# Building the per-batch matrix M four batches at a time, from stacked high and low weights, instead of in one fold per batch

## The chip, the core and the metric

The kernel runs on one core of one Trainium2 chip. The metric is the device time of one execution, in microseconds, as a median of several. Engines are called as the profile calls them: PE (TensorE) with PEld, its weight loads; DVE (VectorE); ACT (ScalarE); POOL (GpSimd); SP (SyncE), which issues every DMA here.

## What is computed

```python
ctx = x + _L0_xattn_ref(ctx_1024, _layernorm(x), fside, fside, ln1_w, ln1_b, ln2_w, ln2_b, Wq, Wkv, Wout)
#   q = ln2(layernorm(x)) @ Wq, scaled and shifted per head;  k, v = split(ln1(ctx_1024) @ Wkv)
#   out = softmax(q k^T / 8) v @ Wout,   16 heads of 64, 64 context rows per batch
y   = ctx + tanh(((_layernorm(ctx) @ W) @ A1) @ A2 + bias)
```

x is 16 batches x 1024 rows x 512, all float32. Each operand of a matmul is split in two float32r parts, high (`_hi`) and low (`_lo`), and a product is made of the passes high x high, high x low and low x high.

## The kernel before, in words

Once, in a setup, the weights are loaded and split, the three FFN matrices are multiplied into one (W3), and the keys and values of all 16 batches are computed and stored to DRAM (`kv_scratch`). For each batch b two matrices stand in SBUF: M = Wq K^T (512 x 1024, so that x M gives the scores of all heads at once) and N = V Wout (1024 x 512). Both are kept as high and low parts.

The work on x goes in slots. Slot t treats one tile of 128 rows, `m = t % 8` is its place in the batch, and there are T = 128 slots and three more to drain. In one slot PE does, in program order (`slot_pe`): the scores of tile t in two halves q = 0, 1, 12 matmuls of 128x512 each (`passes`, L153 and L158); the FFN of tile t-3, 12 matmuls (L153, L158, operands x2T and W3); and the product of the softmaxed scores of tile t-1 with N, two halves of 12 (L848, L855). That is 60 matmuls. Between the scores and their use lies a chain over all engines: DVE adds the bias (L923) and takes the maximum (L928), POOL subtracts it (L1021), ACT takes the exponential (L868), DVE sums (L934, L937), POOL normalises (L1028), SP stores the result to `p_scratch` (L782) and reads it back with rows and columns exchanged (`p_moved`, L791), DVE transposes 32x32 blocks (L949), ACT and DVE split into `pT_hi` (L873) and `pT_lo` (L954). The row tile after the attention goes a like way (`x2_scratch` L766, `x2_moved` L778, L961, L878, L970). Every queue runs its own program in order, and semaphores tie them together. SP is a queue like the others: a DMA that waits holds up all behind it.

Two slots of a batch do more. In slot m = 0, PE makes N of this batch (`fold_n_pe`, 24 matmuls), from the block-diagonal values in `bdv`. In slot m = 7, M of the next batch is made (`fold_m_pe`), strewn between the other matmuls: 16 chunks c, each of two head pairs, each pair one matmul of 256 columns (L658, Wq_hi with the high and low keys side by side) and one of 128 (L659, Wq_lo with the high keys), into one of four PSUM banks c % 4. ACT takes the high part out (L671) and copies the cross term (L670), DVE makes the rest (L681) and for odd chunks the low part (L684), POOL the low part of even ones (L691). PE may use a bank again only when these have read it (`m_bank_read`). There is one M buffer, so that the old M must be done with first. The keys are laid block-diagonally into `bdk` at m = 4, the values into `bdv` at m = 6 (L609, L618, L600).

Slots 0 to 2 and the last 8 stand written out; the 15 x 8 between them are a hardware loop over batches (`run`, L1055), with DMA addresses and wait values from registers.

```python
            for t in range(3):
                slot(eng, t, t)
            with eng.Fori(0, B - 1) as b:
                for j in range(3, TPB + 3):
                    slot(eng, b * TPB + j, j % TPB)
            for t in range(T - 5, T + 3):
                slot(eng, t, t % TPB)
```

## Time and profile before

| | |
|---|---|
| median of 3 runs | 2175.47 us (2173.73 to 2175.64) |
| the profiled execution, its own time | 2175.19 us |
| its span | 2173.3 us |
| mean granted clock of PE | 0.989 |
| PE / PEld busy | 97% / 80% |
| DVE / ACT / POOL busy | 77% / 60% / 60% |
| DMA | 342.80 MB, mean 158 GB/s; share of the 16 engines 50.4% |

The span is what the profile covers; 1.9 us of the execution's own time lie outside of it. Two matmuls overlap in the records (each is shown with 0.39 us, though one starts every 0.227 us), so PE's pace is read from the starts, not from the durations.

### The profile page before, as it was taken

To read this page: it belongs to the slowest core of one execution; us is meant where nothing else is said; L and a number is where in the kernel's file an instruction comes from. 1 tells how busy PE (TensorE), PEld (TensorE's weight loads), DVE (VectorE), ACT (ScalarE), POOL (GpSimd) and SP (SyncE) were. 2 spreads that over 40 slices of the span, in tenths; PEclk is the share of its full clock that TensorE was granted. 3 is DMA by queue.
4 is the path that set the end of the run, shared out by engine and by line. 5 is a ranking of instruction groups with operands and counts; after the bars stand their busy time and mean duration, and the time that the engine had idled before them with its cause. 6 is when DMAs were issued, how large, how long until landed. Compare 5 with 4: busy or idle time off the path is not lost.

```text
span 2173.3 us, 35341 instructions
## 1 busy us (share of the span) xinstructions
PE 2104.7 (97%) x9632; PEld 1744.9 (80%) x9632; DVE 1678.3 (77%) x2778; ACT 1309.2 (60%) x3095; POOL 1306.3 (60%) x1460
## 2 busy tenths in 40 slices
PE   6977999999999999999999999999999999999997
PEld 5766888888888888888888888888888888888886
DVE  6746787878787787878878777878778787878875
ACT  3344666666666666666666666666666666665654
POOL 4433656656565666656565665756565666666564
PEclk8998999999999999999999999999999999999999
DMA  6422545555454544546464545546464555545453
GB/s 210 155 88 82 178 146 168 158 159 175 140 183 136 182 155 158 175 145 187 126 183 140 181 152 164 173 144 184 133 183 149 162 166 154 179 136 183 135 175 126
DMA packets 379887, 342.80 MB, mean 158 GB/s; under 512 B 72273, under 2 KB 269137, under 8 KB 379857
## 3 DMA queue, kind: packets, MB, share of 16 engines
q1 hardware_dynamic: 379856, 342.45, 50.4%
q8 instruction: 13, 0.21, 0.0%
q14 instruction: 18, 0.14, 0.0%
HBM read 199.62 MB, written 142.67 MB: 157 GB/s over the span
## 4 chain that ended last, share of the span: by engine, by line
PE 79%; issue 4%; ACT 4%; DVE 3%; POOL 2%; DMA 1%; SPq 0%; ACTq 0%; POOLq 0%; DVEq 0%
PE bank L153 31%; PE bank L848 19%; PE bank L158 15%; PE bank L855 10%; PE bank L658 3%; POOL area L1021 1%; ACT pT_hi L873 1%; PE bank L659 1%; DVE pT_lo L954 1%; ACT M_hi L671 1%; DVE row_max L928 1%; DVE turned L949 1%; ACT bank L718 1%; ACT area L670 0%; DMA p_moved<-p_scratch 0%
## 5 line engine op out<-in xcount | busy, mean ns | idle before, releaser
L1021 POOL TENSOR_TENSOR area<-area,row_max 128x256 f32<-128x256 f32 x512 | 360.2, 725 | 536.7 <-DVE row_max L928 536.7
L868 ACT ACTIVATE area<-area 128x512 f32<-128x512 f32 x256 | 162.0, 633 | 434.2 <-POOL area L1021 434.2
L1028 POOL TENSOR_TENSOR area<-area,row_inv 128x512 f32<-128x512 f32 x256 | 319.2, 1265 | 171.0 <-DVE row_inv L937 171.0
L848 PE MATMUL bank<-N_hi,pT_hi 128*128 128x512 f32 x1024 | 401.0, 392 | 4.1 <-ACT pT_hi L873 4.0
L153 PE MATMUL bank<-M_hi,xT_hi 128*128 128x512 f32 x1024 | 399.5, 390 | 0.0
L153 PE MATMUL bank<-M_lo,xT_hi 128*128 128x512 f32 x1024 | 399.2, 390 | 0.0
L848 PE MATMUL bank<-N_lo,pT_hi 128*128 128x512 f32 x1024 | 398.9, 390 | 0.0
L923 DVE SCALAR_TENSOR_TENSOR area<-bank,rs,area 128x512 f32<-128x512 f32 x256 | 192.0, 750 | 173.7 <-PE bank L158 170.5
L158 PE MATMUL bank<-M_hi,xT_lo 128*128 128x512 f32 x1024 | 274.8, 390 | 6.1 <-POOL xT_lo L745 5.9
L855 PE MATMUL bank<-N_hi,pT_lo 128*128 128x512 f32 x1024 | 276.1, 391 | 0.0
L954 DVE TENSOR_TENSOR pT_lo<-turned,pT_hi 128x512 fp32r<-128x512 f32 x256 | 230.2, 899 | 40.0 <-ACT pT_hi L873 40.0
L158 PEld LDWEIGHTS bank<-M_hi,xT_lo 128*128 128x128 f32 x1024 | 192.5, 188 | 46.9 <-POOL xT_lo L745 6.3
L848 PEld LDWEIGHTS bank<-N_hi,pT_hi 128*128 128x128 f32 x1024 | 192.2, 188 | 45.3 <-issue 4.2
L153 PEld LDWEIGHTS bank<-M_hi,xT_hi 128*128 128x128 f32 x1024 | 192.8, 188 | 40.4
L153 PEld LDWEIGHTS bank<-M_lo,xT_hi 128*128 128x128 f32 x1024 | 192.8, 188 | 40.4
L848 PEld LDWEIGHTS bank<-N_lo,pT_hi 128*128 128x128 f32 x1024 | 192.3, 188 | 39.1
L855 PEld LDWEIGHTS bank<-N_hi,pT_lo 128*128 128x128 f32 x1024 | 189.8, 188 | 38.4 <-DVE pT_lo L954 0.5
L153 PE MATMUL bank<-W_hi,x2T_hi 128*128 128x512 f32 x512 | 200.2, 391 | 4.5 <-ACT x2T_hi L878 4.5
L153 PE MATMUL bank<-W_lo,x2T_hi 128*128 128x512 f32 x512 | 200.0, 391 | 0.0
L949 DVE STREAM_TRANSPOSE turned<-p_moved 128x512 f32<-128x512 f32 x256 | 181.3, 708 | 19.5 <-DMA p_moved<-p_scratch 5.5
L722 ACT ACTIVATE bank<-area,st 128x512 f32<-128x512 f32 x256 | 177.3, 693 | 8.4
L718 ACT ACTIVATE bank<-area 128x512 f32<-128x512 f32 x256 | 153.6, 600 | 47.3 <-DVE area L964 42.9
(137 smaller groups left out, 4137.3 us busy)
## 6 DMA issues: line engine op xcount, KB each, us to landing
p_scratch<-area SPq DMA_DIRECT2D x256, 256.0 KB, 2.0
p_moved<-p_scratch SPq DMA_DIRECT2D x1024, 64.0 KB, 2.2
area<-x_dram SPq DMA_DIRECT2D x128, 256.0 KB, 3.1
area<-x_turned_dram SPq DMA_DIRECT2D x128, 256.0 KB, 2.7
x_scratch<-area SPq DMA_DIRECT2D x128, 256.0 KB, 3.3
x_moved<-x_scratch SPq DMA_DIRECT2D x512, 64.0 KB, 1.9
y_dram<-area SPq DMA_DIRECT2D x128, 256.0 KB, 2.1
kv_scratch<-area SPq DMA_DIRECT2D x32, 256.0 KB, 2.1
```

Source lines behind the costliest of these rows:

```text
L153: mm = eng.matmul(ps, sh, mv, start=(n == 0), stop=False)
L158: mm = eng.matmul(ps, sl, mh, start=False, stop=(k == len(pairs) - 1))
L718: act.activation(junk_ps[:], src, ACT.Identity, accum_out=st[:, 0:1]).then_inc(s_sum, 1)
L722: act.activation(junk_ps[:], src, ACT.Square, bias=st[:, 1:2], accum_out=st[:, 2:3]).then_inc(s_sq, 1)
L848: pe.matmul(O_ps[:], pT_hi[:, k * P:(k + 1) * P], n_cols(mv, k), start=(k == 0 and mv is N_hi), stop=False)
L855: mm = pe.matmul(O_ps[:], pT_lo[:, k * P:(k + 1) * P], n_cols(N_hi, k), start=False, stop=(k == 7))
L868: act.activation(s, s, ACT.Exp).then_inc(s_ex[q], 1)
L923: dve.scalar_tensor_tensor(out=half_of(S[m % 2], q), in0=S_ps[q][:], scalar=rs1[:, 0:1], in1=half_of(bias, q), op0=ALU.mult, op1=ALU.add). ...
L949: dve.transpose(turned[:].rearrange("p (k g r) -> p k g r", k=4, g=4), blocks).then_inc(s_pt[q], 1)
L954: dve.tensor_tensor(half_of(pT_lo, q), turned[:], half_of(pT_hi, q).bitcast(F32), ALU.subtract).then_inc(s_pTl[q], 1)
L1021: last = pool.tensor_tensor(s, s, row.to_broadcast([P, 2, 4, J2]), ALU.subtract)
L1028: pool.tensor_tensor(s, s, inv, ALU.mult).then_inc(s_p[q], 1)
```

## The change

- `fold_m_pe` now runs only once, in the setup, and makes M of batches 0 and 1. It makes them in full, with three matmuls of 256 columns per head pair. ACT and DVE split batch 0's part into the first M buffer. Batch 1's part goes raw to DRAM (`m_scratch`), by 16 DMAs.
- There are two M buffers (M0, M1); batch b uses buffer b % 2. `M1` takes the room of Wq.
- In the setup the high and low Wq of one head are stored on top of each other (64 + 64 rows) to `wst_scratch`, by 16 DMAs.
- M of batches 2 to 15 is made in 128 tiles (`tile_pe`), for one head pair and one quarter of the rows at a time: for batches 2 and 3 in 32 tiles of 4 matmuls of 128 columns, then for 4 batches at once in 96 tiles of 4 matmuls of 256 columns. The moving operand is the keys, loaded into both halves of the partitions (`k_raw`), and split by ACT and POOL once for four tiles. A table gives each tile a place (A, B, C, D) in a slot: slots 1 to 8 have A to D, slots 9 to 24 have A and C, slots 25 to 88 have B, later ones none.
- ACT copies each tile from its bank to `evac` (behind `pT_hi` for A and B, behind the layernorm sums for C, at the start of the next slot for D), SP stores it to `m_scratch` and loads the weights of the tile after next.
- In each slot up to t = 119 an eighth of the next batch's M is read back into `land`; ACT (`land_hi`) and POOL (`land_lo`) split it into the other M buffer at the start of the next slot (the last eighth at the end of slot 7).
- The fold of slot m = 7 and the bdk work of m = 4 are gone. The values now go to `bdv` in slot m = 0, just before N is made, by way of `land`.
- No loop: all 131 slots are written out, with constant addresses and waits.

```diff
+        GROUPS = ((2, 2), (4, 4), (8, 4), (12, 4))
+        for m in range(TPB):
+            for i, place in enumerate("ABCD"):
+                tile_at[1 + m, place] = 4 * m + i
+        for m in range(2 * TPB):
+            tile_at[TPB + 1 + m, "A"], tile_at[TPB + 1 + m, "C"] = 32 + 2 * m, 32 + 2 * m + 1
+        for m in range(8 * TPB):
+            tile_at[3 * TPB + 1 + m, "B"] = 64 + m
...
+        def tile_pe(pe, n):
+            nb, ps, _ = tile_bufs(n)
+            pe.wait_ge(s_wst[n % 2], 16 * (n // 2) + 16)
+            pe.wait_ge(s_kl, n // 4 + 1)
+            at_least(pe, s_tev, n)
+            for h in range(2):
+                own = slice(h * nb * CTX, (h + 1) * nb * CTX)
+                st = wst[n % 2][:, h * P:(h + 1) * P]
+                pe.matmul(ps[:, own], st, k_hi[:, own], start=True, stop=False)
+                mm = pe.matmul(ps[:, own], st, k_lo[:, own], start=False, stop=True)
+            mm.then_inc(s_mt, 1)
...
+            act.wait_ge(s_mt, n + 1)
...
+            act.copy(buf.rearrange("p (b h j) -> p h b j", b=nb, h=2), ps.rearrange("p (h b j) -> p h b j", h=2, b=nb)).then_inc(s_tev, 1)
...
+            sp.wait_ge(s_tev, n + 1)
+            sp.dma_start(m_scratch[b0:b0 + nb, dc, p // 4, :, (p % 4) * P:(p % 4 + 1) * P].rearrange("b d c -> d b c"),
+                         buf.rearrange("p (b c) -> p b c", b=nb)).then_inc(s_tw_half[n % 2] if nb == 2 else s_tw, 16)
+            load_wst(sp, n + 2)
...
+        def land_lo(eng, l):
+            eng.wait_ge(s_lh, l + 1)
+            eng.tensor_tensor(m_land(M_lo, l), land_raw, m_land(M_hi, l).bitcast(F32), ALU.subtract).then_inc(s_ll, 1)
...
@@ slot_sp
-            if has["more"] and m == 3:
-                load_k(sp, (t + 5) // 8)
-            if has["more"] and m == 5:
-                load_v(sp, (t + 3) // 8)
+            for kp in first_of_pair(t):
+                load_k(sp, kp + 1)
+            if has["v"]:
+                load_v(sp, t // TPB)
+            if has["land"] and m > 0:
+                load_land(sp, t)
+            store("A")
...
+            store("B")
...
+                store("C")
+                if has["land"] and m == 0:
+                    load_land(sp, t)
                 if fetch:
                     load_xT(sp, t + 2)
...
@@ slot_pe
-                    if has["fold_m"]:
-                        fold_m_pe(pe, t + 1, (0, 1), lambda c: pe.wait_ge(s_sb[c], t + 1))
+            tile("A")
...
-                if has["fold_m"]:
-                    fold_m_pe(pe, t + 1, folds[2 * q])
+                tile("BC"[q])
...
-            for t in range(3):
-                slot(eng, t, t)
-            with eng.Fori(0, B - 1) as b:
-                for j in range(3, TPB + 3):
-                    slot(eng, b * TPB + j, j % TPB)
-            for t in range(T - 5, T + 3):
+            for t in range(T + 3):
                 slot(eng, t, t % TPB)
```

How the instructions stand. On PE, inside the loop, slot m = 7 before, from the end of the FFN's first passes to the first half of the attention (L658 and L659 are the fold, L158 the FFN's last pass, L848 the attention):

```order
L659 MATMUL bank<-bdk,Wq_lo 128x128
L158 MATMUL bank<-W_hi,x2T_lo 128x512 [waits s_x2Tl]
L158 MATMUL bank<-W_hi,x2T_lo 128x512 x3
L658 MATMUL bank<-bdk,Wq_hi 128x256 [waits s_x2]
L659 MATMUL bank<-bdk,Wq_lo 128x128
...
L642 REGISTER_ALU [waits s_mr]
L658 MATMUL bank<-bdk,Wq_hi 128x256 [waits s_mq]
...
L848 MATMUL bank<-N_hi,pT_hi 128x512 [waits s_pTh0]
```

and PE in a slot of the changed kernel that has a tile A, behind the scores (L163 is their last pass, L771 and L772 the tile, L158 the FFN):

```order
L163 MATMUL bank<-M_hi,xT_lo 128x512 x4
L771 MATMUL bank<-k_hi,wst 128x256 [waits s_tev,s_kl,s_wst0]
L772 MATMUL bank<-k_lo,wst 128x256
L771 MATMUL bank<-k_hi,wst 128x256
L772 MATMUL bank<-k_lo,wst 128x256
L158 MATMUL bank<-W_hi,x2T_hi 128x512 [waits s_fb,s_x2Th]
```

The waits on the fold's readers (s_mr, s_mq, s_mlv) are gone from the slots; a tile waits for its weights, for its keys, and for ACT's copy of the tile before.

On SP, one slot of the loop before:

```order
L766 DMA x_scratch<-area 128x512 [waits s_x2]
L778 DMA x_moved<-x_scratch 32x4x128 [waits s_x2w]
L778 DMA x_moved<-x_scratch 32x4x128 x3
L782 DMA p_scratch<-area 128x512 [waits s_p0]
L782 DMA p_scratch<-area 128x512 [waits s_p1]
...
L574 DMA area<-x_turned_dram 128x512
```

and one of slots 25 to 88 after (L744 loads keys, in one slot of four, L819 the eighth of M, L793 stores the tile, L737 loads weights):

```order
L914 DMA x_scratch<-area 128x512 [waits s_x2]
L744 DMA k_raw<-kv_scratch 64x2x256 [waits s_kl]
L744 DMA k_raw<-kv_scratch 64x2x256
L819 DMA land<-m_scratch 128x512 [waits s_ll]
L929 DMA x_moved<-x_scratch 32x4x128 [waits s_x2w]
L929 DMA x_moved<-x_scratch 32x4x128 x3
L793 DMA m_scratch<-evac 128x4x128 [waits s_tev]
L737 DMA wst<-wst_scratch 128x256 [waits s_mt]
L934 DMA p_scratch<-area 128x512 [waits s_p0]
L934 DMA p_scratch<-area 128x512 [waits s_p1]
L620 DMA area<-x_turned_dram 128x512 [waits s_xTl]
```

SP's store of the probabilities now stands behind a DMA that waits for ACT's copy of tile B.

## Rows read from the trace of the kernel before

**Rows 1.** The page, parts 1 and 2: busy time, 40 slices.

```profile
PE 2104.7 (97%) x9632; PEld 1744.9 (80%) x9632; DVE 1678.3 (77%) x2778; ACT 1309.2 (60%) x3095; POOL 1306.3 (60%) x1460
...
PE   6977999999999999999999999999999999999997
```

**Rows 2.** Chain that ended last, in order of time: start us, us, what.

```profile
423.72 1.84 PE bank L153 x8
...
2030.95 1.84 PE bank L153 x8
```

**Rows 3.** Timeline of PE: first matmul of slots m=6, 7, 0 and 3.

```profile
1005.16 0.39 PE L153 MATMUL bank<-M_hi,xT_hi 128*128 128x512 f32 x1
...
1018.76 0.39 PE L153 MATMUL bank<-M_hi,xT_hi 128*128 128x512 f32 x1
...
1041.73 0.39 PE L153 MATMUL bank<-M_hi,xT_hi 128*128 128x512 f32 x1
...
1088.00 0.39 PE L153 MATMUL bank<-M_hi,xT_hi 128*128 128x512 f32 x1
```

**Rows 4.** Timeline of PE inside the fold of slot m=7.

```profile
1026.01 0.28 PE L658 MATMUL bank<-bdk,Wq_hi 128*128 128x256 f32 x1
...
1026.18 0.34 PE L658 MATMUL bank<-bdk,Wq_hi 128*128 128x256 f32 x1
1026.36 0.22 PE L659 MATMUL bank<-bdk,Wq_lo 128*128 128x128 f32 x1
...
1026.88 1.14 PE L158 MATMUL bank<-W_hi,x2T_lo 128*128 128x512 f32 x4
1027.86 0.28 PE L658 MATMUL bank<-bdk,Wq_hi 128*128 128x256 f32 x1
```

**Rows 5.** Timeline of ACT, POOL and SP in slot m=6 (starts 1005.16).

```profile
1011.32 0.63 ACT L868 ACTIVATE area<-area 128x512 f32<-128x512 f32 x1 [3.11 <-POOL area L1021]
...
1014.56 0.60 ACT L873 CAST pT_hi<-turned 128x512 fp32r<-128x512 f32 x1
...
1010.11 1.18 POOL L1021 TENSOR_TENSOR area<-area,row_max 128x256 f32<-128x256 f32 x2 [2.40 <-DVE row_max L928]
...
1017.74 1.29 POOL L745 TENSOR_TENSOR xT_lo<-area,xT_hi 128x512 fp32r<-128x512 f32 x1
...
1014.67 1.74 SPq L778 DMA_DIRECT2D x_moved<-x_scratch  x4
1016.46 1.68 SPq L782 DMA_DIRECT2D p_scratch<-area  x2
1019.19 0.34 SPq L574 DMA_DIRECT2D area<-x_turned_dram  x1
1019.72 3.65 SPq L791 DMA_DIRECT2D p_moved<-p_scratch  x8
```

**Rows 6.** Groups by line and form: xcount | busy us, mean ns | idle before.

```profile
L618 ACT CAST bdv<-area 64x512 fp32r<-64x512 f32 x32 | 19.6, 613 | 0.2
L600 DVE TENSOR_TENSOR bdv<-area,bdv 64x512 fp32r<-64x512 f32 x32 | 29.2, 913 | 13.4 <-ACT bdv L618 13.2
```

**Rows 7.** DMA issues: KB each, median us to landing.

```profile
p_moved<-p_scratch SPq DMA_DIRECT2D x1024, 64.0 KB, 2.2
...
area<-kv_scratch SPq DMA_DIRECT2D x32, 256.0 KB, 3.8
```

**Rows 8.** Timeline of PE at the end of the setup and first waits in slots 1, 2.

```profile
165.48 0.55 PE L658 MATMUL bank<-bdk,Wq_hi 128*128 128x256 f32 x1 [5.04 <-issue]
165.83 0.31 PE L659 MATMUL bank<-bdk,Wq_lo 128*128 128x128 f32 x1
165.94 0.52 PE L658 MATMUL bank<-bdk,Wq_hi 128*128 128x256 f32 x1
...
176.10 0.47 PE L153 MATMUL bank<-M_hi,xT_hi 128*128 128x512 f32 x1
```

More of the change, by code:

```diff
@@ L206, in build @@
         beside[15] += [("factors", 0)]
+        for g in range(4):
+            beside[13 + 2 * g] = beside.get(13 + 2 * g, []) + [("wst", g)]
+        for i, n in enumerate((16, 17, 24, 25)):
+            beside[n] = beside.get(n, []) + [("zero", i)]
         for n in range(4 * PAIRS):
@@ L376, in setup_act @@
                 if step == "k0":
-                    k_prepare_act(act, 0)
+                    act.wait_ge(s_k0in, 16)
+                    act.wait_ge(s_kz, 4)
+                    for half in range(2):
+                        last = act.copy(k0_diag(0, half), k0_dense(half))
+                    last.then_inc(s_k0h, 1)
                 if step == "x0":
@@ L617, in v_prepare_act @@
             for half in range(2):
-                last = act.copy(diag(bdv, 0, half), dense(kvf, half))
+                last = act.copy(diag(bdv, 0, half), dense(land, half))
             last.then_inc(s_vh, 1)
@@ L762, in slot_sp, with store @@
             has = parts(t, m)
-            fetch = not isinstance(t, int) or t + 2 < T
+            fetch = t + 2 < T
+            def store(place):
+                if (t, place) in tile_at:
+                    tile_store(sp, tile_at[t, place])
             if has["x2"]:
@@ L791, in slot_sp @@
                         sp.dma_start(dst, src).then_inc(s_pr[q], 16)
+            store("D")
             if has["ffn"]:
@@ L800, in slot_pe, with tile @@
             has = parts(t, m)
-            first = isinstance(t, int) and t == 0
+            first = t == 0
+            M_hi_now, M_lo_now = M_hi[t // TPB % 2], M_lo[t // TPB % 2]
+            def tile(place):
+                if (t, place) in tile_at:
+                    tile_pe(pe, tile_at[t, place])
             if has["scores"]:
@@ L906, in slot_act @@
                 act.activation(hid, hid, ACT.Tanh).then_inc(s_th, 1)
-            if has["fold_m"]:
-                m_act(act, t + 1, range(10, 16))
+            if has["land"] and m == 7:
+                land_hi(act, t)
             if has["fold_n"]:
@@ L913, in slot_dve @@
             has = parts(t, m)
-            first = isinstance(t, int) and t == 0
+            first = t == 0
             r2 = (m - 2) % RING
@@ L1042, in slot_pool @@
                 pow1(pool, t + 1)
+            if has["land"] and m == 7:
+                land_lo(pool, t)
             if has["x2"]:
```

369 lines of the change are left out of this document (226 added, 143 removed).

## Prediction

> **What bounds the kernel now.** I read the page first: PE is busy for 97% of the span, and all slices but the first few are full [rows 1]. So the next question is whether it is PE's own work that sets the pace, or waits hidden in overlapping records. The chain of waits in order of time answers it for the batch: the first 8 matmuls of a score stand at 423.72 and, 13 batches later, at 2030.95 [rows 2]. A batch takes 1607.23 / 13 = **123.63 us**, each time. The timeline answers it for the slot. Slot m = 6 runs from 1005.16 to 1018.76, 13.60 us [rows 3], and has 60 matmuls of 512 columns: one per 0.2267 us, with nothing between. From m = 0 to m = 3 it is 1088.00 - 1041.73 = 46.27 us; three slots and the 24 matmuls of N are 3 x 13.60 + 5.44 = 46.24. So these run without a gap too, and the loop's jump, which lies just before m = 3, costs PE nothing. What is left of a batch is slot m = 7: 1041.73 - 1018.76 = 22.97 us, or 9.37 above a plain slot. In a batch, 123.63 - 8 x 13.60 - 5.44 = **9.39 us** are the fold of M.
>
> Where the 9.39 go: 32 head pairs. Four pairs start at 1026.01 and the next wide matmul at 1026.88; the four wide ones behind them take 0.98 us where 0.91 is usual [rows 4]. That is 0.94 us for four pairs, 0.235 for a matmul of 256 and one of 128 columns, 7.5 us for 32. The other 1.9 us are PE's waits for the readers of the four banks.
>
> **What goes.** 15 folds stand in slots (for batches 1 to 15; the one for batch 0 is in the setup): 15 x 9.39 = **-140.9 us**, pace and waits together. The readers of the banks on ACT, DVE and POOL go too, which by itself is worth nothing, since PE has no gap elsewhere.
>
> **What PE gets.** 128 tiles of 4 matmuls. No row shows two 256-column matmuls behind each other. By columns, half of a wide one is 0.113 us; by the pair, 0.235 / 2 = 0.117 for the mean of a 256 and a 128. That a 128 costs as much as a 256 in this mean (0.170 us would be the pair by columns) says that short ones are held up by something other than their columns, of about 0.117 us, which the 256 nearly covers. The dearest reading is the distance of starts, 0.18 us from the 256 to the 128 at 1026.18 [rows 4]; I don't take it, since the 128 behind it then takes only 0.06 and the pair stays 0.235. So 0.117 for both forms: 128 x 4 x 0.117 = **+59.9 us**. Bounds: 96 x 4 x 0.113 + 32 x 4 x 0.057 = 50.7 below, 96 x 4 x 0.18 + 32 x 4 x 0.117 = 84.1 above.
>
> The Trainium skill ("TensorE: Matmul & The Clock Gate", on the back-to-back gap and on LDWEIGHTS) has columns / 2.4 + 2.5 ns for a matmul and columns / 1.2 for a weight load: 109 ns for 256 columns, 107 for the load. By it the tiles would be 96 x 4 x 0.109 + 32 x 4 x 0.107 = 55.6 us, an estimate 4 us below mine. The trace has 227 ns where that rule has 216, so I stay with the rows.
>
> **What the slot's other engines get.** The chain from scores to probabilities must not get longer than its slack. In slot m = 6 (all times now from its start at 1005.16): ACT's second pT_hi starts at 9.40 and ends at 10.0, while PE comes to it behind 48 matmuls, at 10.88. **Slack 0.88 us** [rows 5], the smallest I found. A slot with tiles is 0.47 us longer per tile, which adds to it.
>
> POOL: one `land_lo` per slot, at the price of L745, 1.29 us, before the subtraction. POOL waits 2.40 us before that, until 4.95 [rows 5]. ACT can do `land_hi` behind the layernorm sums, about 3.1 to 3.7, so `land_lo` runs 3.7 to 5.0: 0.05 late. In a slot with a key split (another 0.6 on ACT and 1.29 on POOL, from 2.6 on) it is some 0.5 late. Both are below the slack: nothing.
>
> ACT: `land_hi` and a tile's copy, 0.6 each. It waits 3.11 us before the exponential [rows 5]; the copies stand behind pT_hi. Nothing.
>
> SP: its issues cost 0.34 to 0.45 each. In a plain slot: `x_moved` 9.51 to 11.25, `p_scratch` from 11.30 (the second part waits for POOL until about 12.6), then L574, held by xT_lo until 14.03, then `p_moved` from 14.56 [rows 5], that is 0.96 into the next slot. Changed: the store of tile B waits for a copy that ends at about 10.6, so it goes out at 11.25, with the weights until 11.95; the first `p_scratch` is 0.65 late, the second and L574 not at all, `p_moved` starts at 14.6 as before. With place C the store waits for a copy behind the layernorm sums: in slots 9 to 24 PE ends tile C at 11.8 and the copy is out at 12.7, in slots 1 to 8 at 12.3 and 13.0. Store and weights end by 13.7, ahead of 14.03. So **nothing**, but with 0.3 us to spare: here the change is nearest to a cost. In slots 1 to 8, SP's issues come to 7.8 + 4 x 0.7 + 1.1 = 11.7 of 15.5 us.
>
> DMA: 15 x 2.1 MB of M written and read, 16.8 of weights, 8 of keys: about 85 MB on 342.80. A landing of 2.2 us [rows 7] may become 2.5. `p_moved` has 1.4 us before pT_hi needs it. Nothing.
>
> **The values in slot m = 0.** They are loaded at about 6.1 and land 3.8 us later [rows 7], at 9.9. ACT lays them out in 2 x 0.61 us, DVE in 2 x 0.91 [rows 6], behind pT_lo, which ends at about 11.7: ready at 13.7. PE wants them at 13.60, or later in a slot with tiles. The high parts of N then start 0.5 us later than before on ACT. I take 0.2 us x 15 = **+3 us**, from 0 to 10 (0.7 each, all of a late load).
>
> **Setup.** The fold has 96 matmuls of 256 where 64 short ones were. It begins at the low pace: a pair in 0.46 - 0.03 = 0.43 us [rows 8], 0.21 each. 24 at 0.21 and 72 at 0.117 are 13.5 us against the 10.6 from 165.48 to 176.10: +2.9. Batch 1's parts are stored by SP, which still has its bias stores and loads to do, and the four raw buffers wait for landings: +2. The two-batch key block doubles ACT's and DVE's work in a stretch where PE waits anyway for that chain: 1.2 + 1.4 = +2.6. The weight stores and POOL's four memsets: +0.5. Sum **+8 us**, from 3 to 16. In slots 1 and 2 the tiles fill waits that PE has as the pipe fills: -1.
>
> **Sum.** Against the profiled execution's 2175.2 us (its span of 2173.3 and 1.9 around it; 0.3 below the median of 2175.47): -140.9 + 59.9 + 3 + 8 - 1 = -71.0, so **2104 us**, 3.3% less.
>
> **The loop.** It goes, and by the row at 1088.00 this is worth nothing to PE. The Trainium skill ("Runtime: NRT & Kernel Launch", on instruction fetch) says that a jump out of the fetched pages stalls its engine until the target is loaded, and that straight code streams. This would make the change better than my sum: 14 jumps of a DMA landing, 2.2 us, are 31 us, if they cost anything now. The trace has no gap for it.
>
> **Rivals.**
> 1. *Tiles or queues a little dearer.* Either the 256-column matmuls take 0.18 us (+24 us, 2128), or the 0.3 us on SP and 0.88 on ACT are overrun by 0.2 to 0.4 us in the 119 slots with landings (+24 to +48, up to 2152). For: SP has four more issues in a full slot and DMA a quarter more bytes. Against: every place is behind work that waits anyway. I name 2128.
> 2. *Slower than before: SP passes the wait on.* SP has one queue. Where the store of B or C waits for ACT, `p_scratch`, `p_moved` and the next `x2` store all move, ACT's pT_hi of the next slot comes later, so does the next copy, and the loop feeds itself. Break-even is 71 us / 119 slots = 0.6 us per slot beyond all slack. If a store and a weight load (0.7 us) and landings longer by 0.3 us came in full, with no slack used, it would be 1.0 us x 119 = 119 us: 2104 + 119 = 2223. Against: the waits that I count on SP (3.4 us before `x_moved`, 1.0, 1.1) are there in every slot.
> 3. *The loop did cost*, and 31 us more are gained: 2073. Against: 46.27 us for 46.24 of matmuls.
> 4. *The change doesn't do what it says*: PE's waits at the fold move elsewhere, for instance to N in m = 0, 2 us each. 15 x 2 = 30: 2134. For: ACT makes the values, then the sums, then N's high parts. It lies in the range.
>
> **How the numbers follow.** My forecast has a chance of 0.67, rival 1 has 0.16, rival 2 has 0.06, rival 3 has 0.03, rival 4 has 0.05; 0.03 is left for things I don't see. Its own bounds (50.7 to 84.1 for the tiles, 3 to 16, 0 to 10) give about 2092 to 2125; the range, which must also take in most of rivals 1 and 4, is 2092 to 2140. No case lies near no change, taken as within 0.2%, about what a measurement of this kernel can tell: 0.01. Slower 0.06, faster 0.93.
>
> **What would show it.** The batch from slot 96 on should take 114.3 to 114.5 us, slots 25 to 88 14.07 each, slots 9 to 24 14.54, slots 1 to 8 15.5; no PE wait on ACT's copy of a tile; PE's wait for the values in m = 0 below 0.7 us; the first score at about 184. I am wrong if plain slots are longer than 13.6 us, if `p_moved` is issued later than 1.2 us into a slot, or if DVE waits for it.

## The result, and the profile after

The change makes the kernel slower by 0.4%, little but clear of the noise: **2183.03 us** (median of 14 runs, 2179.06 to 2190.59) against 2175.47 (14 runs, 2173.73 to 2178.22), a ratio of **1.0038** (95% interval 1.003 to 1.0047). The forecast was 2104, so 79 us are missing. The profiled execution took 2187.0 us, with a span of 2185.2; the prediction's account is compared with that one. The folds are gone and the tiles cost about what was expected; the gain went into many short waits.

The page of the changed kernel: busy time, PE's slices, DMA traffic, the chain of work that ended last (shares of the span by engine) and the landing time of `p_scratch`.

```profile
PE 2073.7 (95%) x9216; PEld 1695.5 (78%) x9216; DVE 1517.9 (69%) x2387; ACT 1317.7 (60%) x2985; POOL 1393.6 (64%) x1488
...
PE   6976989999999999999999999999999999999997
...
DMA packets 479502, 432.07 MB, mean 198 GB/s; under 512 B 63200, under 2 KB 353248, under 8 KB 479328
...
SPq 23%; DMA 23%; PE 18%; DVE 9%; issue 7%; POOL 7%; ACT 6%; POOLq 0%; DVEq 0%; ACTq 0%
...
p_scratch<-area SPq DMA_DIRECT2D x256, 256.0 KB, 2.8
```

PE's row of slices looks as full as before [rows 1], and its busy time fell by only 31 us: 416 fewer matmuls. These two rows do not give the reason away. The chain does. On the page of the kernel before it reads:

```profile
PE 79%; issue 4%; ACT 4%; DVE 3%; POOL 2%; DMA 1%; SPq 0%; ACTq 0%; POOLq 0%; DVEq 0%
```

PE no longer sets the pace: its share of the chain falls from 79% to 18%, and SP's issues (SPq) with the landings of transfers (DMA) have 46% where they had 1%. The last row fits: a landing of 2.8 us that took 2.0 before, with 432 MB moved instead of 343.

The waits of the changed kernel: us in total, times, longest.

```profile
DVE turned L1124 <- DMA x_moved<-x_scratch: 115.6, 86, 4.5
DVE turned L1112 <- DMA p_moved<-p_scratch: 92.5, 79, 3.5
...
PE bank L1004 <- ACT pT_hi L1032: 22.2, 32, 1.5
...
PE bank L158 <- DVE bdv L639: 17.5, 13, 1.8
```

In the kernel before, DVE waited 5.5 us for `p_moved` (7 times) and 17.4 for `x_moved` (37 times). So the loop from the scores through DRAM to pT (the softmaxed scores, transposed) has used up its slack, and PE waits for its end.

Timeline of PE in the changed kernel: the first matmul of slots 72 (m = 0), 73, 74 and 75.

```profile
1325.85 0.39 PE L158 MATMUL bank<-M_hi,xT_hi 128*128 128x512 f32 x1
...
1347.04 0.39 PE L158 MATMUL bank<-M_hi,xT_hi 128*128 128x512 f32 x1
...
1362.20 0.39 PE L158 MATMUL bank<-M_hi,xT_hi 128*128 128x512 f32 x1
...
1376.30 0.39 PE L158 MATMUL bank<-M_hi,xT_hi 128*128 128x512 f32 x1
```

Slot 74 takes 14.10 us: 13.60 as before [rows 3] and one tile at **0.50**. Slots with two tiles take 14.60. So this is the measure for what follows: 13.60, plus 0.50 per tile, plus 5.44 in m = 0. Slot 72 (21.19) is 1.65 above it, slot 73 (15.16) is 1.06 above. Summed over all slots, for each profiled execution:

```
us above that measure  first score  slots 0-7   m=0    m=1  m=2-6   m=7    sum
                                                (slots from 8 on)
before                   176.1         9.6      0.3    0.0    0.0  131.2  141.1
the change               189.1        12.2     30.2   15.4   15.3    3.7   76.7
v_early                  187.7         6.5     26.2   15.4    7.0    2.0   57.1
m1_order                 189.9         8.7     24.9    0.1   10.7    4.7   49.1
best2                    189.0         8.8     28.1    0.1   12.3    2.6   51.9
act_dma                  190.3         7.9     27.3   16.5    9.2    2.1   63.1
all3                     190.2         9.2     31.4    0.5    9.4    8.3   58.8
store_d                  188.7         9.2     24.4    0.1   19.5    4.5   57.7
store_c_only             191.4         8.1     23.3   15.6    1.6    0.2   48.8
m1_store_c               189.8         9.7     21.7    0.1    4.7    0.5   36.7
late_load                191.5        10.1     51.4    0.1    7.8    0.4   69.8
best3                    191.0        10.2      8.6    0.1    4.2    0.5   23.5
no_store                 189.7        -2.3     17.6   15.7    0.1    0.2   31.3
no_tst                   188.6        -0.1     20.1   15.3    0.8    0.3   36.3
no_wst                   189.7         1.8     23.1   15.4    1.6    0.2   42.1
no_land                  189.3         3.7     21.8    0.1    4.4    1.4   31.3
v_none                   188.8         9.7      2.7   15.4   14.5    0.8   43.0
loop_off                 176.1         9.8      0.3    0.0    1.1  131.7  142.9
extra_sp                 175.4        10.3      0.3    0.0    3.5  140.1  154.2
extra_act                176.0        10.3      0.3    0.0    0.4  132.0  143.0
```

The 131.2 of before are the folds in slots m = 7, fourteen of them; the fifteenth is in slot 7. The table has one execution per kernel, and not always a middling one: `v_early`'s is 9 us below its median and `act_dma`'s 12 below, `v_none`'s is 4 below, the change's 4 and `late_load`'s 5 above, the others about 3 or less away. Between kernels that are the same there, slots 0 to 7 differ by up to 6 us, m = 0 by 5 (24.9 to 30.2), m = 2 to 6 by 8 (7.0 to 15.3), m = 7 by 4 (0.8 to 4.7) and m = 1 by about 1. So only larger differences count, and the medians decide.

A part of the loss is not waiting but a lower clock behind it. Slots 32 and 72 of the change, both m = 0 (window, its us, busy us of PE, PEld, DVE, ACT and POOL, then PE's granted clock, the DMA engines' share and GB/s):

```profile
704.47:727.88 23.41, 21.62 (x90) 17.24 (x88) 15.58 (x24) 14.58 (x31) 12.79 (x15) 0.93 0.78 231
1325.85:1347.04 21.19, 19.89 (x90) 16.16 (x88) 15.91 (x24) 14.32 (x31) 12.81 (x15) 1.00 0.77 225
```

Slot 72 is 1.65 us above the measure, with a wait of PE of 1.30. Slot 32 is 3.87 above it, with a wait of 1.79 for the same values, behind which PE ran for a stretch at the lower level, 1.2 GHz instead of 2.4. From these two slots such a stretch costs about 1.7 us, an estimate. The change has them in slots 2, 7, 24 and 32, as well as in the first two slots; the kernel before has none from 210 to 2160 us.

### The profile page after: what moved, and what is told of

Same layout as the page of the kernel before. It is cut to its first block, busy times and chain, and to the rows that moved or that the text cites. A ratio compares the mean times of both kernels' runs of the same rounds, so it can differ in the third digit from the quotient of the medians.

```text
span 2185.2 us, 31801 instructions
## 1 busy us (share of the span) xinstructions
PE 2073.7 (95%) x9216; PEld 1695.5 (78%) x9216; DVE 1517.9 (69%) x2387; ACT 1317.7 (60%) x2985; POOL 1393.6 (64%) x1488
## 4 chain that ended last, share of the span: by engine, by line
SPq 23%; DMA 23%; PE 18%; DVE 9%; issue 7%; POOL 7%; ACT 6%; POOLq 0%; DVEq 0%; ACTq 0%
SPq L946 11%; DMA x_scratch<-area 9%; DMA p_scratch<-area 8%; PE bank L158 7%; PE bank L1004 5%; SPq L929 4%; PE bank L163 3%; DVE N_lo L858 3%; DMA land<-kv_scratch 2%; PE bank L1009 2%; POOL area L1181 2%; POOL M_lo L838 2%; POOL area L1174 2%; SPq L737 1%; SPq L616 1%
## 5 line engine op out<-in xcount | busy, mean ns | idle before, releaser
L1174 POOL TENSOR_TENSOR area<-area,row_max 128x256 f32<-128x256 f32 x512 | 337.3, 681 | 217.8 <-DVE row_max L1091 217.8
L1004 PE MATMUL bank<-N_hi,pT_hi 128*128 128x512 f32 x1024 | 408.1, 399 | 22.7 <-ACT pT_hi L1032 22.2
L158 PE MATMUL bank<-M_hi,xT_hi 128*128 128x512 f32 x1024 | 401.1, 392 | 4.0 <-POOL M_lo L838 2.8
L158 PE MATMUL bank<-M_lo,xT_hi 128*128 128x512 f32 x1024 | 400.2, 391 | 0.0
L838 POOL TENSOR_TENSOR M_lo<-land,M_hi 128x512 fp32r<-128x512 f32 x120 | 176.9, 1474 | 165.0 <-ACT M_hi L834 164.9
L163 PE MATMUL bank<-M_hi,xT_lo 128*128 128x512 f32 x1024 | 275.7, 391 | 5.9 <-POOL xT_lo L891 5.9
L1117 DVE TENSOR_TENSOR pT_lo<-turned,pT_hi 128x512 fp32r<-128x512 f32 x256 | 213.8, 835 | 71.3 <-ACT pT_hi L1032 70.8
L163 PEld LDWEIGHTS bank<-M_hi,xT_lo 128*128 128x128 f32 x1024 | 193.5, 189 | 46.6 <-POOL xT_lo L891 6.3
L158 PEld LDWEIGHTS bank<-M_hi,xT_hi 128*128 128x128 f32 x1024 | 193.1, 189 | 45.7 <-POOL M_lo L838 4.5
L158 PEld LDWEIGHTS bank<-M_lo,xT_hi 128*128 128x128 f32 x1024 | 193.2, 189 | 39.8
L158 PE MATMUL bank<-W_hi,x2T_hi 128*128 128x512 f32 x512 | 200.8, 392 | 4.4 <-ACT x2T_hi L1037 4.4
L158 PE MATMUL bank<-W_lo,x2T_hi 128*128 128x512 f32 x512 | 200.2, 391 | 0.0
```

The costliest lines, as they stand in the source:

```text
L158: mm = eng.matmul(ps, sh, mv, start=(n == 0), stop=False)
L163: mm = eng.matmul(ps, sl, mh, start=False, stop=(k == len(pairs) - 1))
L838: eng.tensor_tensor(m_land(M_lo, l), land_raw, m_land(M_hi, l).bitcast(F32), ALU.subtract).then_inc(s_ll, 1)
L1004: pe.matmul(O_ps[:], pT_hi[:, k * P:(k + 1) * P], n_cols(mv, k), start=(k == 0 and mv is N_hi), stop=False)
L1117: dve.tensor_tensor(half_of(pT_lo, q), turned[:], half_of(pT_hi, q).bitcast(F32), ALU.subtract).then_inc(s_pTl[q], 1)
L1174: last = pool.tensor_tensor(s, s, row.to_broadcast([P, 2, 4, J2]), ALU.subtract)
```

## The experiments

Eighteen kernels ran. Each median stands against the kernel before of the same chip, whose median lay between 2174.6 and 2175.5 throughout.

**1. Is it the loop?** `loop_off` is the kernel before, its loop written out.

```diff
-            for t in range(3):
-                slot(eng, t, t)
-            with eng.Fori(0, B - 1) as b:
-                for j in range(3, TPB + 3):
-                    slot(eng, b * TPB + j, j % TPB)
-            for t in range(T - 5, T + 3):
-                slot(eng, t, t % TPB)
+            for t in range(T + 3):
+                slot(eng, t, t % TPB)
```

> The kernel before with its hardware loop written out, and nothing else. If straight code costs instruction fetches that hold an engine up, or contends with the data on the DMA engines, it is slower than before: a part of the 80 us that the forecast missed would show here, at least 10 us. If the loop did cost what the skill's rule on jumps says, it is faster by up to 31 us. My theory (the lost time is SP's queue and the order of the work, not the code) has 2175 within 5 us and slots of 13.60 us as before.

2178.37 us (10 runs), ratio 1.0019 (1.0009 to 1.0028). The loop was worth about 3.5 us, the other way than rival 3 had it; 121 of PE's 127 slots are the same to 0.1 us, the others differ by 0.1 to 0.5. A jump that costs PE nothing is what the rows before showed; why straight code is a little slower is open.

**2. Which of the added work costs?** These leave work out of the change. `no_store` makes the tiles and does not store them; it loads weights only twice, and every landing reads batch 1's M. `no_land` has no landings; all batches use the first M.

> The changed kernel in which tiles are computed and copied out of PSUM, but not stored, and their weights are loaded only twice; every landing reads batch 1's M. It leaves out 128 stores and 126 loads on SP, some 50 MB: the output of batches 2 to 15 is not the reference's. Moving the same DMAs to ACT's queue has left the time where it was. If the transfers' own load on the DMA engines is what holds slots 1 to 88 up, the loss there (some 35 us outside of m = 1 and N) goes here though it didn't there: 20 to 30 us faster, 2155. If neither issues nor bytes matter, within 5 us of 2183.

> The changed kernel without the landing: no load of M eighths, no split on ACT and POOL, all batches use the first M. The output of batches 1 to 15 is not the reference's. Stores and weight loads stay. The m = 1 loss (15 us) must go, and 120 loads (31 MB). If only the order on POOL is at stake, 2183 - 20 = 2163, as in the kernel with the changed order; if the landing's bytes count too, down to 2145.

`no_store`: 2142.71 us, ratio 0.9848 (0.9834 to 0.9862). `no_land`: 2145.6, ratio 0.987 (0.9856 to 0.9884). Without stores and weight loads, the losses in m = 2 to 7 and the first eight slots vanish and `p_scratch` lands in 2.0 us; without landings the m = 1 loss vanishes. Two further kernels split the first pair: `no_tst` drops the stores alone (the landings read batch 1's M), `no_wst` the 126 later weight loads (the products use the first two tiles' weights).

> The change without the stores of the tiles to m_scratch: products, copies and weight loads stay, and the landings read batch 1's M for every batch. If the stores are what the slots m=2 to 6 and the first batches lose to, the time comes near that of no_store (2142.7; 2143 to 2150) and p_scratch lands in 2.0 to 2.2 us; if the weight loads are, it stays within 8 us of 2183.

> The change without the 126 later loads of weights (128 KB each, on SP, behind each tile's store); the products use the first two tiles' weights throughout. If the weight loads are as much to blame as the stores, it gains 12 to 25 us on 2183; if the stores are, under 8.

2149.4 us, ratio 0.989 (0.9873 to 0.9908), and 2150.83, ratio 0.9881 (0.9866 to 0.9896). I had asked which of the two is to blame: either one taken away ends the loss in m = 2 to 6 (0.8 and 1.6 us are left). Even `no_land`, which takes away a third issue and leaves these two, has only 4.4 us there, with `p_scratch` still landing in 2.8 us. That is how slack runs out. Each is an issue of 0.4 to 0.5 us on SP, and the slots don't have room for all. Issue and bytes go together in these four kernels; the order of the same issues is tried below.

`v_none` leaves out the values' work in slot m = 0 of batches 1 to 15; every batch uses the values of batch 0.

> The change without the values' work in slot m=0 of batches 1 to 15: no load of V, no product with the new V, no copy and no subtraction into bdv's lower half; every batch uses the values of batch 0. Everything else is as in the change. It bounds what the values cost in m=0 when the fold's products no longer cover them. If they are the loss of the m=0 slots, these fall from 30 us over the plain slot's time to under 8 us and the median goes to 2155 to 2163; if it is the doubled tile work (two stores in m=0 as in every slot), under 10 us are gained.

2157.47 us, ratio 0.993 (0.9915 to 0.9945). The m = 0 slots lose 2.7 us instead of 30.2, so the values are that loss, with the clock behind their waits.

**3. The m = 1 slots: `m1_order`.** POOL splits the landed part of M between the halves of the subtraction instead of ahead of both.

```diff
-            for l in landed_in(t):
-                land_lo(pool, l)
+            if m != 1:
+                for l in landed_in(t):
+                    land_lo(pool, l)
             if has["scores"]:
                 subtract_maximum(0)
+                if m == 1:
+                    for l in landed_in(t):
+                        land_lo(pool, l)
                 subtract_maximum(1)
```

> The changed kernel with POOL's landing split of slot m = 1 between the two halves of the subtraction instead of before the first. 14 slots m = 1 are 1.1 us longer than their matmuls. If this is POOL's 1.29 us ahead of the first subtraction, which in m = 1 begins later because DVE has made N's low parts, nearly all of it goes: 12 to 15 us faster. If it is the late start of slot m = 1 itself (N's splits), below 3 us.

2162.62 us (7 runs), ratio **0.9951** (0.9937 to 0.9965), and the m = 1 loss of 15 us is gone; the other 5 us in the median lie within the scatter. The change's timeline of DVE, ACT and POOL in slot 73 (from 1347.04):

```profile
1343.32 5.24 DVE L858 TENSOR_TENSOR N_lo<-bank,N_hi 128x512 fp32r<-128x512 f32 x8 [1.17 <-ACT N_hi L853]
1348.47 0.70 DVE L1124 STREAM_TRANSPOSE turned<-x_moved 128x512 f32<-128x512 f32 x1
...
1352.19 0.67 DVE L1091 TENSOR_REDUCE row_max<-area 128x8 f32<-128x512 f32 x1
...
1352.29 0.60 ACT L834 CAST M_hi<-land 128x512 fp32r<-128x512 f32 x1
1355.43 0.63 ACT L1027 ACTIVATE area<-area 128x512 f32<-128x512 f32 x1 [2.54 <-POOL area L1174]
...
1352.97 1.29 POOL L838 TENSOR_TENSOR M_lo<-land,M_hi 128x512 fp32r<-128x512 f32 x1 [1.25 <-ACT M_hi L834]
1354.21 2.33 POOL L1174 TENSOR_TENSOR area<-area,row_max 128x256 f32<-128x256 f32 x4
```

And POOL and ACT in slot 73 of `m1_order` (from 1327.56):

```profile
1333.45 1.19 POOL L1174 TENSOR_TENSOR area<-area,row_max 128x256 f32<-128x256 f32 x2 [1.22 <-DVE row_max L1091]
1334.60 1.30 POOL L838 TENSOR_TENSOR M_lo<-land,M_hi 128x512 fp32r<-128x512 f32 x1
...
1334.67 0.64 ACT L1027 ACTIVATE area<-area 128x512 f32<-128x512 f32 x1 [1.26 <-POOL area L1174]
```

In m = 1, DVE has just split N and turns `x_moved` only 1.43 us into the slot; ACT, and so `land_hi`, follow. The row maximum was there at 1352.86, and POOL came to it at 1354.21. The first exponential starts 8.39 us into the slot, with the new order 7.11.

**4. SP's queue.** `extra_sp` and `extra_act` add one 256 KB store per slot, in 512-byte pieces, to `loop_off`; nobody reads it. It is issued on SP ahead of `p_scratch`, or on ACT behind pT_hi.

```diff
+            if 3 <= t < 120:
+                extra_store(sp, t)
             if has["scores"]:
                 for q in range(2):
                     sp.wait_ge(s_p[q], t + 1)
```

> The kernel before with its loop written out (2178.4) and one more transfer in each of slots 3 to 119, issued on SP ahead of the stores to p_scratch: 256 KB from SBUF to DRAM in 512-byte pieces, which nobody reads; no product, no copy, no load. This is the DMA load of a tile by itself. If the transfers' load is what costs the change its slots, each m=0 slot grows by over 0.5 us and the whole by 10 to 30 us (2188 to 2208), with p_scratch's landing at 2.4 to 2.8 us. If the cost came from TensorE's and ACT's side of the tiles, the time stays within 4 us of 2178.

> The same transfer issued from ACT's queue, behind the second half of pT_hi, so that SP issues what it did before. If the load on the DMA engines is the cause, the loss is within 5 us of that with SP; if SP's time for the issue is, the loss is gone (within 4 us of 2178).

`extra_sp`: 2188.07 us (4 runs), ratio 1.0057 (1.0042 to 1.0073), `p_scratch` landing in 2.7 us. `extra_act`: 2177.43, ratio 1.001 (1.0001 to 1.002), landing in 2.1. The same bytes cost 10 us over `loop_off` on the one queue and nothing on the other, where they also leave earlier: 9.30 us into the slot instead of 11.78. So the queue and the place in time are not told apart. And the sum came as expected, but not the place: 8.4 of the 10 us are in the slots m = 7, with their fold, 2.4 in m = 2 to 6 and none in m = 0. By itself one such store on SP hardly costs a plain slot anything. The Trainium skill ("DMA: Bandwidth & Descriptors", on issuing engines not being separate queues) says that DMAs issued by different engines run on the same 16 DMA engines, and another issuer saves only the sequencer's time. Here the issue takes 0.44 us on SP and 0.38 on ACT, and what it costs depends on what stands behind it; no run separates the saving that the page names from the place.

Moving the change's own stores and weight loads to ACT's queue, behind each copy (`act_dma`), should then have helped:

> The changed kernel with the tile stores and the weight loads issued by ACT instead of SP, same bytes, same tiles. In the changed kernel's slots 25 to 88 (m = 2 to 7) 17.5 us are lost over 14.10 us each, in slots 1 to 7 about 12. If SP's serial chain (store x2, landing, x2 read, tile store and weights, p store, landing, p read) sets these, most of it goes: 15 to 30 us faster than the changed kernel, about 2160. If it is the DMA engines' load (65% busy against 50%), the bytes are the same and it stays within 5 us of 2183. ACT pays some 0.1 to 0.9 us per tile and has it to spare.

2186.98 us, only 4 runs from 2174.62 to 2193.43, ratio 1.0065 (1.0042 to 1.0089). The median did not fall. The profiled execution is the fastest of the four, so its trace says little of the median: in it `p_scratch` still lands in 2.6 us, and m = 2 to 6 lose 9.2 us, which the scatter of that column covers. Why is open: no run separates ACT's issue time (0.39 and 0.52 us behind each tile) from the transfers' new place in time.

What did help is SP's order. The change's timeline of SP for slot 74 (from 1362.20, the next slot from 1376.30):

```profile
1368.27 0.45 SPq L914 DMA_DIRECT2D x_scratch<-area  x1
1368.76 0.43 SPq L819 DMA_DIRECT2D land<-m_scratch  x1
1372.20 1.74 SPq L929 DMA_DIRECT2D x_moved<-x_scratch  x4
1373.98 0.43 SPq L793 DMA_DIRECT2D m_scratch<-evac  x1
1374.46 0.51 SPq L737 DMA_DIRECT2D wst<-wst_scratch  x1
1375.01 0.96 SPq L934 DMA_DIRECT2D p_scratch<-area  x2
1376.74 0.33 SPq L620 DMA_DIRECT2D area<-x_turned_dram  x1
1379.49 0.79 SPq L946 DMA_DIRECT2D p_moved<-p_scratch  x2
```

`x_moved` is issued 10.00 us into the slot (before 9.51), the first `p_scratch` 12.81 (before 11.30), `p_moved` **3.19 into the next slot** (before 0.96) [rows 5]. Over the 40 slots m = 2 to 6 between 25 and 88 the means are 7.36 for `x_scratch` (before 5.80), 11.10 for `x_moved` (before 9.27), 13.96 for `p_scratch` (before 11.23) and 2.72 for `p_moved` (before 0.99). Behind `p_scratch` SP waits 2 us or more for the landing: that is where another issue is free. `store_c_only` is the change with just this:

```diff
-            store("B")
+            if t < 25:
+                store("B")
...
                 store("C")
+                if t >= 25:
+                    store("B")
```

> The change with one edit: in slots 25 to 104 tile B's store and the next weights are issued behind the stores to p_scratch instead of ahead of them. If SP's order is the cause of what slots m=2 to 7 of that stretch lose (17.5 us) and of a part of the m=0 slots' loss, 2183 falls by 14 to 22 us to 2161 to 2169, with the m=1 slots still 1.1 us each over. If it only worked together with m1_order, by under 8.

2162.71 us (5 runs), ratio **0.9948** (0.9936 to 0.9961), all five below the fastest of the change. Tile B ends with slot 88, so no later slot has this edit. In its profiled execution m = 2 to 6 lose 1.6 us instead of 15.3, m = 7 0.2 instead of 3.7 and m = 0 23.3 instead of 30.2. The 4 us less in slots 0 to 7, which have no edit, are scatter. Bytes and issues are the same as in the change, so their order is what costs. `m1_store_c` has `m1_order` too:

> m1_order (2162.6), and in slots 25 to 104 SP issues tile B's store and the next weights behind the stores to p_scratch, where it waits about 3 us for these to land (1355.4 to 1358.9 in slot 74 of m1_order), instead of ahead of them, where the first of them is 0.9 us late (POOL was done at 1353.2, the store is issued at 1354.08). If SP's order is what slots 25 to 104 lose, their m=2 to 6 lose under 4 us instead of 8.6 and their m=0 slots some too: 2150 to 2157. If it is the load on the DMA engines, within 4 us of 2162.6. store_d, which moved them further, behind p_moved, made it worse.

2148.21 us (4 runs), ratio **0.9877** (0.9862 to 0.9892). SP in slot 74 of `m1_store_c` (from 1332.01):

```profile
1342.19 1.74 SPq L929 DMA_DIRECT2D x_moved<-x_scratch  x4
1343.98 1.22 SPq L935 DMA_DIRECT2D p_scratch<-area  x2
1345.25 1.29 SPq L793 DMA_DIRECT2D m_scratch<-evac  x1
1346.58 0.51 SPq L737 DMA_DIRECT2D wst<-wst_scratch  x1
1347.13 0.44 SPq L620 DMA_DIRECT2D area<-x_turned_dram  x1
1347.68 3.73 SPq L949 DMA_DIRECT2D p_moved<-p_scratch  x8
```

`p_scratch` goes out at 11.97, `p_moved` 1.57 into the next slot, and over the 40 slots 12.12 and 1.29, with `x_scratch` at 6.35. `p_scratch` also lands in 2.2 us again. Whether the earlier issue or the shorter landing does it, the next kernel bears on. `store_d` moved the same two issues behind `p_moved` instead (with `m1_order` and `v_early`):

> v_early and m1_order together, and in slots 25 to 104 tile B's store and the load of the next weights stand behind the reads of p_moved on SP instead of ahead of the stores to p_scratch. If the transfers of a store slow down only what is issued just behind them, p_scratch's half-stores land again as in the kernel before (2.0 us instead of 2.8), slots m=2 to 6 of that stretch lose less than 3 us in all instead of 11.8, and the median falls to 2150 to 2156. If what counts is the sum of the DMA work of a slot, or a store that is late for its buffer, it stays within 4 us of 2164.2. That kernel alone had 2164.2.

2171.77 us (11 runs), ratio 0.9989 (0.998 to 0.9998): worse than without (`best2`, 2164.24), and m = 2 to 6 lose 19.5. `p_scratch` lands in 2.2 us, but is still issued at 14.02 (`best2` 14.15): behind `p_moved` nothing waits, so every issue there delays the next `x_scratch`, which goes out at 7.85 (`best2` 7.51) and now has the store's transfers just ahead of it: it lands in 4.3 us on the mean of those slots instead of 3.7. A short landing of `p_scratch` is thus not enough. My expectation that getting out from in front of `p_scratch` is all that counts was wrong.

**5. The values in m = 0.** `v_early` issues the values' load in slot m = 7, between the halves of `p_moved`:

```diff
-            if has["v"]:
-                load_v(sp, t // TPB)
...
                 for q in range(2):
+                    if q == 1 and m == 7 and t + 1 < T:
+                        load_v(sp, (t + 1) // TPB)
                     sp.wait_ge(s_pw[q], 16 * t + 16)
```

> The changed kernel with the load of a batch's values issued in slot m = 7 between the two halves of p_moved, instead of in slot m = 0 behind the x2 store. Slots m = 0 lose 27 us in all against a forecast of 3. If the late landing (issued 8.3 us into the slot, landed at 12.5) is the cause, 10 to 18 us come back; the rest is the split on ACT and DVE, which has no cover at that place. If the splits alone are the cause, below 3 us.

2174.83 us (10 runs, 2166.08 to 2184.79), ratio 1.0009 (0.9997 to 1.0021): 6 us better than the change by the ratios, 8 by the medians. The m = 0 slots of its profiled execution, the fastest, lose 26.2 us instead of 30.2, no more than the scatter. Together with `m1_order` it added nothing (`best2`: 2164.24, ratio 0.9952, 0.9937 to 0.9968), and with `act_dma` besides it was worse (`all3`: 2170.24, ratio 0.9976, 0.9965 to 0.9986).

> The changed kernel with both edits that helped: the values' load early, and POOL's landing split of slot m = 1 behind the first half of the subtraction. Alone they gave 8 and 20 us of 2183. If they cure different waits they add up: about 2155, against 2175 of the kernel before. If both only take away the same backlog of the queues, it stays at 2162.

> best2 and the tile stores and weight loads issued by ACT. If SP's issues cost anything once the other two are cured, below best2 by 5 to 10 us. If the landings of the transfers, not SP's issue time, hold the slots up, the same as best2 within 5 us or a little slower (ACT pays for the issues).

The reason is in the rest of the chain. SP, ACT, DVE and PE in slot 72 of the change (from 1325.85):

```profile
1333.60 0.43 SPq L634 DMA_DIRECT2D land<-kv_scratch  x1
...
1337.80 1.25 ACT L655 CAST bdv<-land 64x512 fp32r<-64x512 f32 x2 [0.50 <-DMA land<-kv_scratch]
...
1339.08 2.28 DVE L639 TENSOR_TENSOR bdv<-land,bdv 64x512 fp32r<-64x512 f32 x2 [1.12 <-ACT bdv L655]
...
1341.41 0.50 PE L158 MATMUL bank<-Wo_hi,bdv 128*128 128x512 f32 x1 [1.30 <-DVE bdv L639]
```

ACT had been free for only 0.50 us when the values landed, so an earlier load gains 0.5 at most in such a slot. `best3` is `m1_store_c` with `v_early` and an earlier copy and subtraction:

```diff
                 xT_split_hi(act, t + 1)
+            if has["v"]:
+                v_prepare_act(act, t // TPB)
...
-            if has["v"]:
-                v_prepare_act(act, t // TPB)
...
-            if has["scores"]:
+            if has["scores"] and not has["v"]:
                 inverse_sums(1)
             if has["attn"]:
                 pT_lo_part(1)
             if has["v"]:
                 diag_lo(dve, bdv, s_vh, s_vp, t // TPB)
+                inverse_sums(1)
```

> m1_store_c, and the values of the next batch earlier in three places: their load in slot m=7 between the halves of p_moved, ACT's copy behind xT's in slot m=0, DVE's subtraction behind pT_lo's second half but ahead of the second inverse sums. If the m=0 slots wait for this chain (land 1793.69, copy 1794.94, subtraction 1797.64, 1.2 us of PE's wait in slot 104), they lose under 15 us in all instead of 23, and the median is 6 to 12 us under m1_store_c. If the inverse sums, late by 3 us, make p_scratch late for slot m=1, no gain, and slots m=1 lose over 5 us.

**2136.28 us** (5 runs, 2135.68 to 2138.84), ratio **0.9824** (0.981 to 0.9837): 39 us less than before, 47 less than the change. The m = 0 slots lose 8.6 us. `best3` in slot 72 (from 1291.04), ACT, DVE and PE:

```profile
1299.01 1.24 ACT L655 CAST bdv<-land 64x512 fp32r<-64x512 f32 x2
...
1302.15 1.11 DVE L1120 TENSOR_TENSOR pT_lo<-turned,pT_hi 128x512 fp32r<-128x512 f32 x1 [0.57 <-ACT pT_hi L1035]
1303.18 1.38 DVE L639 TENSOR_TENSOR bdv<-land,bdv 64x512 fp32r<-64x512 f32 x2
...
1305.14 0.39 PE L158 MATMUL bank<-Wo_hi,bdv 128*128 128x512 f32 x1
```

The copy is done 2.9 us before the subtraction begins, and PE doesn't wait. `late_load` puts only the load back:

> best3 (2136.3) with the values' load back where the change has it, at the start of slot m=0's program on SP. In m1_order they land 11.6 us into slot 104, 0.9 us after ACT was free for the copy in its old place; the new place is a microsecond or two ahead of that. If the load's place carries the gain, ACT now stands waiting for the land ahead of exp's second half and the time goes back to 2144 to 2156; if the places of the copy and the subtraction carry it, it stays within 4 us of 2136.

2176.13 us (12 runs), ratio 1.0008 (0.9996 to 1.002): not 8 to 20 but 40 us worse, and the m = 0 slots lose 51.4. ACT, DVE and PE in its slot 72:

```profile
1325.51 1.25 ACT L655 CAST bdv<-land 64x512 fp32r<-64x512 f32 x2 [2.60 <-DMA land<-kv_scratch]
...
1328.03 0.69 DVE L1120 TENSOR_TENSOR pT_lo<-turned,pT_hi 128x512 fp32r<-128x512 f32 x1 [3.16 <-ACT pT_hi L1035]
...
1327.98 0.50 PE L1007 MATMUL bank<-N_hi,pT_hi 128*128 128x512 f32 x1 [1.38 <-ACT pT_hi L1035]
```

ACT stands in front of the landing with the second exponential and pT_hi queued behind it. Some of the waits have the lower clock behind them. Slots 72 and 96 of `late_load`:

```profile
1315.05:1336.40 21.35, 19.97 (x89) 16.08 (x88) 14.25 (x24) 13.77 (x30) 12.29 (x15) 1.00 0.64 185
1675.69:1699.83 24.14, 21.00 (x86) 16.83 (x85) 14.80 (x23) 13.59 (x29) 12.64 (x15) 0.93 0.53 159
```

PE waited 1.38 us for pT_hi in the first and 3.14 in the second, and ran at 1.2 GHz for a stretch behind it; eight of the fifteen m = 0 slots have such a stretch, each behind a wait of PE of 1.8 to 3.3 us, while two slots with waits of 1.9 and 2.2 have none. At 1.7 us each these are about 14 of the 51.4 us, an estimate. The load's new place gains little or nothing by itself (`best2` over `m1_order`: nothing); it is what permits the copy's.

## Why the prediction was wrong

Against 2104, the profiled 2187 has 83 us more: first score 5, tiles 4, slots 0 to 7 13, m = 0 slots 27, m = 1 15, m = 2 to 6 15, m = 7 4.

- **What bounds the kernel, what goes, the loop: right.** No slot pays for a fold any more. The loop's 0 was 3.5 us, against the change.
- **Tiles: right in kind, small by 4 us.** 0.50 us each, 64 us in all, where 59.9 was forecast. Starts stand 0.12 apart for 256-column matmuls, and narrow tiles cost the same.
- **Setup: 8 was 13.** The first score stands 13.0 us later than before. The timeline of PE:

```profile
171.95 0.55 PE L691 MATMUL bank<-bdk,M_hi 128*128 128x256 f32 x1 [4.91 <-issue]
...
175.29 0.41 PE L691 MATMUL bank<-bdk,M_hi 128*128 128x256 f32 x1
...
175.81 0.28 PE L691 MATMUL bank<-bdk,M_hi 128*128 128x256 f32 x1
175.92 0.28 PE L692 MATMUL bank<-bdk,M_hi 128*128 128x256 f32 x1
...
189.06 0.58 PE L158 MATMUL bank<-M_hi,xT_hi 128*128 128x512 f32 x1 [1.15 <-ACT xT_hi L886]
```

The fold starts 6.5 us later than before [rows 8], where 3.1 was forecast (2.6 for the key block, 0.5 for the weight stores), and takes 17.1 us, where 13.5 of matmuls and 2 for batch 1's stores were. The pace at its start (0.21) and then (0.12) were right. PE's waits in it are 3.2 us: 1.4 and 0.7 for DVE's work on the banks (ACT and DVE themselves wait 5.1 us for batch 1's stores to land) and 1.2 for xT_hi. Most of the miss, 3.4 us, lies ahead of the fold, and no run shows which part of that work it is.

- **"So nothing, but with 0.3 us to spare" (SP): the step that failed first.** It forecast `p_moved` 14.6 us from the slot's start, as before; the mean is 17.2, 2.72 into the next slot. It took `x_moved` at its old time and added only issues. But the issues of one slot delay the next `x_scratch` (7.36 instead of 5.80), whose landing (3.7 us instead of 3.3) holds `x_moved`. Also the DMA term, "Nothing", was guessed on the landings of `p_moved` (2.2, unchanged), not on the stores (2.0 to 2.8). A chain that closes on itself within one slot has its delay only once if it has slack; without slack it carries it on. This is rival 2's mechanism at a fraction of its price: the change loses 19 us in m = 2 to 7, and `store_c_only` gives back 17 of them (20 us in the median, with a part of m = 0).
- **"Both are below the slack: nothing" (POOL): failed in m = 1.** The times were read in slot m = 6. In m = 1 DVE comes from N, and `land_lo` stands 1.3 us in the way (1.47 on the mean of all, where L745's 1.29 was taken). `m1_order` shows the 15 us of m = 1.
- **"+3 us" for the values in m = 0: it was 30.** The load was put at 6.1 us into the slot and is at 7.75; it lands at 11.95, not 9.9; DVE takes 2.28, not 1.82; ready at 15.5, not 13.7, with PE's wait at 1.30. DVE's price per half, 913 ns in rows 6, is 1112 ns here. In slots 24 and 32 the lower clock came behind it, a term the prediction doesn't have. `v_none` shows 27 us, `best3` gives back 21.6.
- **The first eight slots: -1 was +12.** The prediction added up SP's issues there (11.7 of 15.5 us) but not when the weights land. PE waits for them, all six times in these slots:

```profile
PE bank L771 <- DMA wst<-wst_scratch: 8.3, 6, 2.8
```

The longest of these waits, 2.76 us in slot 7, again has the lower clock behind it (0.84 on the mean of the slot). These slots lose nothing without the stores (`no_tst`, where PE waits 1.7 us for weights) and hardly anything without the weight loads (`no_wst`): four tiles a slot on the same queue. A fix there was not tried.

The test written down beforehand worked: `p_moved` later than 1.2 us into a slot, and DVE waiting for it. It is not sharp: `extra_sp` has `p_moved` at 1.58 on the mean and its plain slots stay near 13.6 us. The chance of 0.93 for faster was too sure. Three zeros, each with less than a microsecond of slack in a slot that repeats 119 times, were taken as independent certainties.

What is left in `best3` over 2104 (32 us): the setup 7, tiles 4, the first eight slots 11, the rest 10.

## What to carry to other kernels

When work off the critical engine is added to a loop whose slack is below 1 us, follow one full turn of the loop through every queue, in each kind of slot, and not only in the plainest one. An issue belongs where its queue waits for a landing anyway: 0.9 us of issues behind `p_scratch` instead of ahead of it was worth 14 us (with `m1_order`) to 20 us, and behind `p_moved` it cost 7.5. Removing a large block also uncovers what ran beside it: move all links of such a chain (load, copy, subtraction), since the load alone gave nothing that shows with `m1_order`, the two others alone cost 28, and all three won 12. And look at PE's granted clock behind its waits: some of a loss may be the clock.

## What was not expected of the hardware

- The same subtraction into the values' block takes DVE 0.69 us per half in `best3` and 1.14 in slot 72 of the change (2.28 for two). In `best3` POOL is idle from 1302.71 to 1305.65 around it; in the change POOL works on SBUF from 1336.36 to 1340.12. The Trainium skill ("SBUF — State Buffer", on who interferes with whom) says that a tensor_tensor with both inputs in SBUF contends with GpSimd's reads by an exclusive lock; the traces agree: the first half, which begins while POOL works, takes 1.58 us, the second, behind POOL's end, 0.69.
- Either of two small transfers (128 or 256 KB) taken away restores `p_scratch`'s landing only to 2.3 us, both together to 2.0, and a move of both behind it to 2.2. Without the 31 MB of `land` (`no_land`) it stays at 2.8. In these runs it is the neighbours in time that lengthen a landing, as much as the sum.
- Kernels that have used up their slack scattered more: the change by 11.5 us over 14 runs and `v_early` by 18.7 over 10, the kernel before by 4.5 over 14 and `loop_off` by 4.3 over 10. `best3` had 3.2, over 5 runs only.
